# Pre-LN attention and binarized feed-forward on one core: probabilities weigh the normalised rows, projection last, rows turned by DMA and VectorE

## Chip, cores and metric

One NeuronCore of a Trainium2 chip runs the whole program. The metric is the device time of one execution in microseconds (us), lower is better. TensorE is called PE below (PEld is its weight load), VectorE DVE, ScalarE ACT, GpSimd POOL, SyncE SP (the engine that issues most DMAs).

## The reference, cut to what matters

```python
def attn(x, Wq, bq, Wk, bk, Wv, bv, Wo, bo):          # x is the layer-normed input
    Q, K, V = x @ Wq.T + bq, x @ Wk.T + bk, x @ Wv.T + bv
    s = einsum('bqd,bkd->bqk', Q, K) / sqrt(d) * gaussian_mask   # a factor per key
    return einsum('bqk,bkd->bqd', softmax(s), V) @ Wo.T + bo
def ffn(x, w1, b1, w2, b2):                            # alpha = mean |w| of a row
    h = gelu(x @ (alpha1 * sign(w1)).T + b1)           # exact gelu
    return h @ (alpha2 * sign(w2)).T + b2
x = x + attn(layernorm(x), ...)
x = x + ffn(layernorm(x), ...)       # x: 16 x 1024 x 256 float32, hidden 1024
```

## The kernel before

There are B = 16 batches of S = 1024 tokens with D = 256 features. Token p*8+t lies in partition p of row tile t, so T = 8 tiles of 128 tokens make a batch, in N2 = 2 halves of TH = 4. C = 2 chunks of 128 features, J = 8 chunks of 128 hidden units. All products run in fp32r, and the precision comes from splitting an operand into a high part (a rounded copy, names with h) and a low part (value minus high, names with l): three products hi*hi, hi*lo, lo*hi, or two where the other side is a sign.

Weights are folded once: M = Wq.T Wk (scores are x M x.T) and N = Wv.T Wo.T (values and output projection in one). Per batch:

- `turn_rows` (PE, L840) transposes the normalised rows into PSUM; ACT and DVE split them into xh, xl (`hi_rows`, `lo_rows`), DVE makes the masked keys from the same PSUM (`mask_keys`, L589), ACT and POOL split these (`hi_keys`, `split_keys` L315).
- `queries` (L856 to L859) and `values` (L873 to L875, rows times N).
- `scores` (L889) of one query tile over all keys; DVE takes the row maximum (`row_max`, L609), ACT the exponential (L447) into the buffer prob, SP issues four DMAs that exchange blocks of 32 partitions (`regroup_probs`), DVE finishes the transpose in 32x32 blocks (`turn_probs`, L615), ACT makes pth (`hi_probs`, L460), POOL ptl (`lo_probs`, L322).
- `weigh_values` (L907 to L909) for each query tile: 24 products with the probabilities as weights, 256 or 258 columns; the two columns more are ones and give the sum of the probabilities. DVE divides and adds (`add_attention`), takes the statistics, POOL the rstd (`rstd_ffn`), ACT normalises again (`normalize_ffn`).
- `turn_rows_ffn` (L935), hi and lo parts (L643), the first feed-forward layer (L1075) by hidden chunk over all 1024 tokens, gelu (ACT, L552) into one of three slots of g, `split_column` (DVE: a copy L648 into gh, a subtraction L650 into gl), the second layer `ffn_rows` (L927, L928), `scale_outputs` (DVE, L668), `add_ffn` (POOL, L340), store.

The order on every engine is written out by hand in a function `batch` per engine; engines meet only at semaphores, and an engine does nothing out of order. Batches overlap: the scores of batch b+1 run between the feed-forward rows of batch b. In `batch` of PE the eight chunks of the first layer stand together and are followed by `scores(b + 1, 0)`. POOL's order behind the last `rstd_ffn` is `add_b2` (eight additions, L334), then `add_ffn` in turn with `add_bias` of the next batch (L328).

## Time and profile before

| what | value |
|---|---|
| median of 3 runs | 1490.33 us (1489.58 to 1492.18) |
| span of the profiled execution (first to last instruction) | 1486.6 us |
| PE busy | 1460.9 us, 98% of the span |
| DVE, ACT, POOL busy | 1030.6, 787.6, 835.7 us (69%, 53%, 56%) |
| chain that ended last | PE 91% of the span |
| mean granted TensorE clock | 0.995 of full speed |

The span is that of one execution that the profiler recorded; it has no run time of its own beside it, and stands 3.7 us under the median of the other three. The chain of waits is followed back from the last instruction, so its shares say which engine set the time where. Matmuls are pipelined: a matmul's own duration is longer than the distance from one to the next, and the distance is what it costs.

### The profile page before, as it was taken

How to read it: one execution, taken by the hardware profiler on the slowest of the kernel's cores; microseconds unless marked ns; L12 is line 12 of the kernel's file. 1: busy time of each engine (PE TensorE's matmuls, PEld its weight loads, DVE VectorE, ACT ScalarE, POOL GpSimd, SP SyncE). 2: the span in 40 equal slices, each digit the busy share in tenths (PEclk: the TensorE clock that was granted, in tenths of full speed). 3: DMA queues.
4: the chain of work that ended last, by engine and by line, in shares of the span. 5: the costliest groups of instructions: out<-in, count | busy, mean ns of one | idle time of the engine just before them, and what ended most of it. 6: DMA issues, size and time to landing. Idle time of an engine off the chain costs nothing.

```text
span 1486.6 us, 24033 instructions
## 1 busy us (share of the span) xinstructions
PE 1460.9 (98%) x9421; PEld 1327.1 (89%) x9421; DVE 1030.6 (69%) x1681; ACT 787.6 (53%) x951; POOL 835.7 (56%) x1097
## 2 busy tenths in 40 slices
PE   8999999999999999999999999999999999999997
PEld 6889989999898998989999898998989999899986
DVE  7567776767767667776776767677675777767574
ACT  5564654646556464654646556465564646546341
POOL 3564637556374673637656375673646746375553
PEclk9999999999999999999999999999999999999999
DMA  5312412223121332403214122231303224121220
GB/s 191 81 34 43 128 27 75 71 57 114 36 76 60 71 100 43 123 19 73 86 48 124 29 71 72 65 106 44 100 29 82 89 44 128 25 75 44 57 86 29
DMA packets 86060, 106.16 MB, mean 71 GB/s; under 512 B 9390, under 2 KB 77372, under 8 KB 85948
## 3 DMA queue, kind: packets, MB, share of 16 engines
q1 hardware_dynamic: 85920, 104.63, 25.0%
q8 instruction: 74, 1.21, 0.4%
q14 instruction: 38, 0.31, 0.1%
q10 hardware_dynamic: 28, 0.01, 0.0%
HBM read 20.72 MB, written 16.78 MB: 25 GB/s over the span
## 4 chain that ended last, share of the span: by engine, by line
PE 91%; DMA 2%; DVE 2%; ACT 2%; SPq 1%; issue 1%; POOL 1%; POOLq 0%
PE ps L889 22%; PE ps L1075 15%; PE ps L927 8%; PE ps L928 8%; PE ps L907 7%; PE ps L909 7%; PE ps L908 7%; PE ps L873 2%; PE ps L874 2%; PE ps L875 2%; PE ps L935 2%; PE ps L856 2%; PE ps L857 2%; PE ps L859 2%; PE ps L840 2%; DMA prob<-prob 2%
## 5 line engine op out<-in xcount | busy, mean ns | idle before, releaser
L322 POOL TENSOR_TENSOR ptl<-pt,pth 128x512 fp32r<-128x512 f32 x256 | 327.1, 1299 | 188.3 <-ACT pth L460 188.3
L907 PE MATMUL ps<-vh,pth 128*128 128x258 f32 x1024 | 293.6, 287 | 2.9 <-POOL ptl L322 2.9
L340 POOL TENSOR_TENSOR xin<-xin,ys 128x256 f32<-128x256 f32 x128 | 94.6, 740 | 353.4 <-DVE ys L668 353.3
L909 PE MATMUL ps<-vh,ptl 128*128 128x258 f32 x1024 | 288.9, 282 | 0.0
L908 PE MATMUL ps<-vl,pth 128*128 128x256 f32 x1024 | 288.4, 282 | 0.0
L460 ACT ACTIVATE pth<-pt 128x1024 fp32r<-128x1024 f32 x128 | 135.8, 1061 | 251.2 <-DVE pt L615 251.1
L927 PE MATMUL ps<-sgn,gh 128*128 128x256 f32 x1024 | 248.6, 284 | 6.1 <-DVE gl L650 6.1
L928 PE MATMUL ps<-sgn,gl 128*128 128x256 f32 x1024 | 248.5, 284 | 0.0
L609 DVE TENSOR_REDUCE nmax<-ps 128x1 f32<-128x1024 f32 x128 | 156.5, 1223 | 120.1 <-PE ps L889 120.1
L447 ACT ACTIVATE prob<-ps,nmax 128x1024 f32<-128x1024 f32 x128 | 142.8, 1115 | 181.6 <-DVE nmax L609 181.4
L615 DVE STREAM_TRANSPOSE pt<-prob 128x1024 f32<-128x1024 f32 x128 | 158.8, 1241 | 67.4 <-DMA prob<-prob 67.2
L927 PEld LDWEIGHTS ps<-sgn,gh 128*128 128x128 f32 x1024 | 197.4, 193 | 7.9 <-issue 6.7
L907 PEld LDWEIGHTS ps<-vh,pth 128*128 128x128 f32 x1024 | 194.2, 190 | 7.4 <-issue 3.3
L908 PEld LDWEIGHTS ps<-vl,pth 128*128 128x128 f32 x1024 | 195.6, 191 | 3.7
L928 PEld LDWEIGHTS ps<-sgn,gl 128*128 128x128 f32 x1024 | 197.5, 193 | 1.2
L909 PEld LDWEIGHTS ps<-vh,ptl 128*128 128x128 f32 x1024 | 195.0, 190 | 0.0
L552 ACT ACTIVATE g<-ps,cols,alpha 128x1024 f32<-128x1024 f32 x120 | 145.2, 1210 | 64.2 <-PE ps L1075 63.6
L889 PE MATMUL ps<-kh,qh 128*128 128x512 f32 x512 | 159.2, 392 | 1.8 <-ACT sgn L430 1.8
L650 DVE TENSOR_TENSOR gl<-g,gh 128x1024 fp32r<-128x1024 f32 x128 | 157.8, 1233 | 4.4
L889 PE MATMUL ps<-kl,qh 128*128 128x512 f32 x512 | 158.7, 391 | 0.0
L889 PE MATMUL ps<-kh,ql 128*128 128x512 f32 x512 | 158.3, 390 | 0.0
L1075 PE MATMUL ps<-x2h,sgn 128*128 128x512 f32 x480 | 154.7, 393 | 0.3
(116 smaller groups left out, 2798.0 us busy)
## 6 DMA issues: line engine op xcount, KB each, us to landing
prob<-prob SPq DMA_DIRECT2D x512, 128.0 KB, 3.1
xin<-in_L_attn_x_dram SPq DMA_DIRECT2D x32, 512.0 KB, 4.5
out_dram<-xin SPq DMA_DIRECT2D x31, 512.0 KB, 3.8
w1s<-in_L_ffn_w_dram SPq DMA_DIRECT2D x1, 1024.0 KB, 10.0
w2s<-in_L_ffn_w_dram SPq DMA_DIRECT2D x1, 1024.0 KB, 12.0
mask_bc<-mask_dram SPq DMA_DIRECT2D x1, 512.0 KB, 7.1
out_dram<-xin SPq DMA_DIRECT2D x1, 384.0 KB, 2.4
wk<-in_L_attn_Wk_dram SPq DMA_DIRECT2D x1, 256.0 KB, 4.8
```

The lines of the kernel that those rows point to most:

```text
L322: pool.tensor_tensor(ptl[:, q % P_SLOTS, half(n)], pt[:, q % P_SLOTS, half(n)], pth[:, q % P_SLOTS, half(n)].bitcast(F32), ALU.subtract).t ...
L552: act.activation(two(g[:, j % G_SLOTS, :]), slot(2 - j % 2), ACT.Gelu, bias=cols[:, j:j + 1], scale=alpha1[:, j:j + 1]).then_inc(gelu_set, 1)
L609: dve.tensor_reduce(nmax[:, q:q + 1], slot(q % 2), mybir.AxisListType.XY, ALU.max, negate=True).then_inc(max_set, 1)
L615: dve.transpose(pt[:, q % P_SLOTS, :].rearrange("p (j g c) -> p g j c", j=T, c=QUAD), regrouped(q).rearrange("p (g j r) -> p g j r", j=T, ...
L650: dve.tensor_tensor(lo, val, hi.bitcast(F32), ALU.subtract).then_inc(gl_set, 1)
L889: last = pe.matmul(ps[:, 2 * (q % 2) + n, :], part[:, c, tile(q)], keys[:, c, half(n)], start=c == 0 and part is qh and keys is kh, stop=c ...
L907: pe.matmul(with_sum, pth[:, q % P_SLOTS, tile(j)], vh[:, j, 0:D + 2], start=j == 0, stop=False)
L908: pe.matmul(bank, pth[:, q % P_SLOTS, tile(j)], vl[:, j, :], start=False, stop=False)
L909: last = pe.matmul(with_sum, ptl[:, q % P_SLOTS, tile(j)], vh[:, j, 0:D + 2], start=False, stop=j == T - 1)
L927: pe.matmul(bank, gh[:, t, j, :], sgn2[:, j, :], start=j == 0, stop=False)
L928: last = pe.matmul(bank, gl[:, t, j, :], sgn2[:, j, :], start=False, stop=j == J - 1)
L1075: last = pe.matmul(ps[:, 4 - 2 * (j % 2) + n, :], sgn1[:, c, tile(j)], x2l[:, n, c, :] if lo else x2h[:, c, half(n)], start=c == 0 and not ...
```

## The change

**Attention.** The values disappear: `weigh_rows` weighs the normalised rows themselves (xnh, xnl as weights, the probabilities of four query tiles as 512 moving columns), and `project` multiplies the result with N afterwards. The sums of the probabilities come from the exponential's accumulator (rsum).

**Rows.** The normalised rows are no longer turned by PE. POOL normalises the rows of batch b+2 (`normalize_attention`), SP issues eight DMAs that regroup them (`regroup_rows`), DVE turns them in 32x32 blocks into SBUF (`turn_rows`). `lo_rows` and `mask_keys` of DVE now read this SBUF copy in place of PSUM, and several operations write or read with a step of four elements (`from_quads`). POOL gets `lo_values` (the low part of the rows).

**Feed-forward.** The first layer goes by pairs of hidden chunks over half of the tokens (`hidden_pair`), the first half before the second half of the attention output is projected. The three slots of g hold both gelu outputs and exponentials, so that `exponentials(b + 1, 0)` waits until the last pair of batch b is split. The second layer uses banks of its own rows in `probs`.

Core of the diff:

```diff
@@ sync
+            def regroup_rows(b, n):
+                sp.wait_ge(xn1_set, T * b + TH * (n + 1))
+                if b == 1:
+                    sp.wait_ge(q_summed, QG)
+                else:
+                    sp.wait_ge(hidden, J * (b - 1))
+                for i in range(QUADS):
+                    sp.dma_start(regrouped_rows[i * QUAD:(i + 1) * QUAD, n, :],
+                                 xn1[:, n, i, :, :, :].rearrange("p c t k -> p (c t k)")).then_inc(rows_back[n], 16)
...
+                if b + 2 < B:
+                    for n in range(N2):
+                        load(b + 2, n)
+                    for n in range(N2):
+                        regroup_rows(b + 2, n)
+                if b + 1 < B:
+                    for q in range(TH):
+                        regroup_probs(b + 1, q)
@@ gpsimd
+            def normalize_attention(b):
...
+                    pool.tensor_scalar(xn1_tile(t), in_blocks(xin[s][:, t, :]), mv1[:, t, 0:1], rstd1[:, t:t + 1],
+                                       ALU.subtract, ALU.mult).then_inc(xn1_set, 1)
+            def lo_values(b):
+                for k in range(QG):
+                    n, c = divmod(k, C)
+                    pool.wait_ge(xnh_set, QG * b + k + 1)
+                    pool.tensor_tensor(rows_by_tile(xnl, n, c), xn1_by_tile(b, n, c),
+                                       rows_by_tile(xnh, n, c).bitcast(F32), ALU.subtract).then_inc(xnl_set, 1)
...
+                for q in tiles_of(1):
+                    rstd_ffn(b, q)
+                if more:
+                    lo_values(b + 1)
+                if b + 2 < B:
+                    normalize_attention(b + 2)
+                add_b2(b)
@@ scalar
             def exponentials(b, q):
                 act.wait_ge(max_set, T * b + q + 1)
-                if b > 0 or q >= 2:
-                    act.wait_ge(p_back[(q - 2) % QUEUED], 64 * ((T * b + q - 2) // QUEUED + 1))
+                if q >= G_SLOTS:
+                    act.wait_ge(p_back[(q - G_SLOTS) % QUEUED], 16 * QUADS * ((T * b + q - G_SLOTS) // QUEUED + 1))
+                elif b > 0:
+                    act.wait_ge(gl_set, J * b)
@@ vector
+            def turn_rows(b, n):
+                dve.wait_ge(rows_back[n], 16 * QUADS * b)
+                dve.wait_ge(kl_set, N2 * b)
+                dve.transpose(rows_t(n).rearrange("p (j g r) -> p g j r", g=QUADS, r=QUAD), ...
@@ tensor
+            def weigh_rows(b, n, steps):
+                parts = [(xv, lo, j) for j in range(T) for xv, lo in ((xnh, 0), (xnl, 0))]
+                parts += [(xnh, 1, j) for j in range(T)]
...
+                        pe.wait_ge(pth_set, T * b + TH * (n + 1))
...
+                        last = pe.matmul(ps[:, PV_BANK + c, :], xv[:, j, tile(c)],
+                                         probs[:, lo, first:first + TH, tile(j)],
+                                         start=k == 0, stop=k == len(parts) - 1)
...
+            def batch(b, more):
+                for i in range(TH):
+                    scores(b, TH + i)
+                    weigh_rows(b, 0, range(6 * i, 6 * i + 6))
+                if more:
+                    queries(b + 1)
+                project(b, 0, more)
+                weigh_rows(b, 1, range(0, 16))
+                turn_rows_ffn(b, 0)
+                weigh_rows(b, 1, range(16, 24))
+                hidden_pair(b, 0)
+                project(b, 1, more)
+                hidden_pair(b, 1)
+                hidden_pair(b, 2)
+                turn_rows_ffn(b, 1)
+                hidden_pair(b, 3)
+                if more:
+                    scores(b + 1, 0)
+                for k in range(4, J):
+                    hidden_pair(b, k)
...
+                scores(b + 1, 1)
+                ffn_row(b, 0, more)
+                ffn_row(b, 1, more)
+                scores(b + 1, 2)
+                ffn_row(b, 2, more)
+                ffn_row(b, 3, more)
+                scores(b + 1, 3)
+                for r in range(TH, T):
+                    ffn_row(b, r, more)
```

`queries(b + 1)` issues its four groups one behind the other into two banks, a group k >= 2 waits for `ql_set` of group k - 2, and `project(b, 0)` takes the same two banks. In the DVE order `row_max(b + 1, 1)`, two `scale_outputs`, `turn_probs(b + 1, 0)`, `row_max(b + 1, 2)`, ..., `turn_probs(b + 1, 2)`, `scale_outputs(b, 4)` follow the last split; `ffn_row(b, 6)` waits for `scale_outputs(b, 4)`.

How the instructions move on POOL, between the last rstd of a batch and the first addition of a feed-forward row. Before:

```order
L315 TENSOR_TENSOR kl<-kmf,kh 128x2x512
L304 TENSOR_TENSOR ve<-mv,eps 128x1
L306 TENSOR_TENSOR rstd<-ve,mhalf 128x1
L309 TENSOR_SCALAR nmr<-mv,rstd 128x1
L334 TENSOR_TENSOR xin<-xin,b_bc 128x256 x8
L340 TENSOR_TENSOR xin<-xin,ys 128x256
```

Now:

```order
L384 TENSOR_TENSOR ve<-mv,eps 128x1
L386 TENSOR_TENSOR rstd<-ve,mhalf 128x1
L389 TENSOR_SCALAR nmr<-mv,rstd 128x1
L365 TENSOR_TENSOR xnl<-xn,xnh 128x4x128 x4
L358 TENSOR_SCALAR xn<-xin,mv,rstd 128x8x32 x8
L402 TENSOR_TENSOR xin<-xin,b_bc 128x256 x8
L409 TENSOR_TENSOR xin<-xin,ys 128x256 x2
```

Twelve instructions (L365, L358) stand in front of the eight additions, and `add_bias` (L328) went to another place.

The same stretch on DVE, from the low part of the feed-forward rows to the next row maximum. Before (the last of the copies and subtractions follow in the same manner):

```order
L643 TENSOR_TENSOR x2l<-ps,x2h 128x1024 [waits x2h_set]
L604 TENSOR_TENSOR vl<-ps,vh 128x512 [waits vh_set]
L648 CAST gh<-g 128x8x128 [waits gelu_set,kl_set]
L650 TENSOR_TENSOR gl<-g,gh 128x8x128 [waits gh_set]
L648 CAST gh<-g 128x8x128 [waits gelu_set]
L650 TENSOR_TENSOR gl<-g,gh 128x8x128 [waits gh_set]
```

Now:

```order
L719 CAST probs<-g 128x2x4x128 [waits gelu_set]
L721 TENSOR_TENSOR probs<-g,probs 128x2x4x128 [waits gh_set]
L712 TENSOR_TENSOR rows_l<-ps,rows_h 128x1024 [waits x2h_set]
L719 CAST probs<-g 128x2x4x128 [waits gelu_set]
L721 TENSOR_TENSOR probs<-g,probs 128x2x4x128 [waits gh_set]
L719 CAST probs<-g 128x2x4x128 [waits gelu_set]
L721 TENSOR_TENSOR probs<-g,probs 128x2x4x128 [waits gh_set]
L677 TENSOR_REDUCE nmax<-ps 128x1 [waits scored]
L719 CAST probs<-g 128x2x4x128 [waits gelu_set]
L721 TENSOR_TENSOR probs<-g,probs 128x2x4x128 [waits gh_set]
```

The low part of the second half of the rows and the first row maximum of the next batch now stand among the copies and subtractions.

## Rows read from the trace of the kernel before

**Rows 1.** The page, part 1 and the clock line of part 2.

```profile
PE 1460.9 (98%) x9421; PEld 1327.1 (89%) x9421; DVE 1030.6 (69%) x1681; ACT 787.6 (53%) x951; POOL 835.7 (56%) x1097
...
PEclk9999999999999999999999999999999999999999
```

**Rows 2.** Timeline of DVE, start us and us, where two batches' splits begin.

```profile
738.39 0.69 DVE L648 CAST gh<-g 128x1024 fp32r<-128x1024 f32 x1 [2.02 <-ACT g L552]
...
740.26 0.69 DVE L648 CAST gh<-g 128x1024 fp32r<-128x1024 f32 x1
...
828.18 0.69 DVE L648 CAST gh<-g 128x1024 fp32r<-128x1024 f32 x1 [2.00 <-ACT g L552]
```

**Rows 3.** The chain of waits in order of time: start us, us, what.

```profile
106.43 13.90 PE ps L1075 x60
...
131.53 2.75 PE ps L889 x12
...
169.04 0.89 PE ps L840 x8
```

**Rows 4.** Timeline of PE: first and last of 23 matmuls of `weigh_values`.

```profile
775.88 0.28 PE L907 MATMUL ps<-vh,pth 128*128 128x258 f32 x1
...
778.50 0.28 PE L908 MATMUL ps<-vl,pth 128*128 128x256 f32 x1
```

**Rows 5.** Timeline: an exponential on ACT, the transpose of its row on DVE.

```profile
777.34 1.12 ACT L447 ACTIVATE prob<-ps,nmax 128x1024 f32<-128x1024 f32 x1 [3.26 <-DVE nmax L609]
...
783.54 1.25 DVE L615 STREAM_TRANSPOSE pt<-prob 128x1024 f32<-128x1024 f32 x1 [0.63 <-DMA prob<-prob]
```

**Rows 6.** Groups of instructions: busy us, mean ns of one, idle before.

```profile
L322 POOL TENSOR_TENSOR ptl<-pt,pth 128x512 fp32r<-128x512 f32 x256 | 327.1, 1299 | 188.3 <-ACT pth L460 188.3
L650 DVE TENSOR_TENSOR gl<-g,gh 128x1024 fp32r<-128x1024 f32 x128 | 157.8, 1233 | 4.4
L609 DVE TENSOR_REDUCE nmax<-ps 128x1 f32<-128x1024 f32 x128 | 156.5, 1223 | 120.1 <-PE ps L889 120.1
L334 POOL TENSOR_TENSOR xin<-xin,b_bc 128x256 f32<-128x256 f32 x128 | 89.8, 740 | 11.4 <-ACT xn L509 10.8 <-DVE xn L638 0.6
L648 DVE CAST gh<-g 128x1024 fp32r<-128x1024 f32 x128 | 87.9, 687 | 31.5 <-ACT g L552 30.1 <-ACT g L493 1.5
L315 POOL TENSOR_TENSOR kl<-kmf,kh 128x1024 fp32r<-128x1024 f32 x32 | 79.7, 2492 | 17.0 <-ACT kh L406 17.0
L306 POOL TENSOR_TENSOR rstd<-ve,mhalf 128x1 f32<-128x1 f32 x128 | 72.6, 567 | 10.0
L596 DVE SCALAR_TENSOR_TENSOR ql<-ps,ccol,qh 128x512 fp32r<-128x512 f32 x64 | 46.5, 747 | 22.4 <-ACT qh L395 22.4
L395 ACT ACTIVATE qh<-ps,ccol 128x512 fp32r<-128x512 f32 x64 | 42.0, 680 | 28.4 <-PE ps L859 28.4
L583 DVE TENSOR_TENSOR xl<-ps,xh 128x1024 fp32r<-128x1024 f32 x32 | 38.4, 1202 | 0.5 <-ACT xh L389 0.5
L309 POOL TENSOR_SCALAR nmr<-mv,rstd 128x1 f32<-128x1 f32 x128 | 34.6, 270 | 12.6
```

**Rows 7.** One batch by stretches: us, then busy us of PE, PEld, DVE, ACT, POOL.

```profile
739.60:829.90 90.30, 90.28 (x588) 82.32 (x587) 63.62 (x104) 49.59 (x59) 51.57 (x68) 1.00 0.24 71
739.60:750.00 10.40, 10.40 (x47) 8.61 (x46) 10.23 (x12) 6.78 (x7) 0.00 (x0) 1.00 0.00 0
```

**Rows 8.** Timeline in the last batch, POOL and DVE at work together.

```profile
1444.81 0.69 DVE L648 CAST gh<-g 128x1024 fp32r<-128x1024 f32 x1
...
1444.90 3.98 POOL L322 TENSOR_TENSOR ptl<-pt,pth 128x512 fp32r<-128x512 f32 x2
...
1445.53 2.20 DVE L650 TENSOR_TENSOR gl<-g,gh 128x1024 fp32r<-128x1024 f32 x1
```

**Rows 9.** Stretches around PE's first long wait; behind POOL's column the granted clock.

```profile
47.90:50.80 2.90, 0.06 (x1) 0.01 (x1) 2.90 (x7) 2.17 (x2) 1.39 (x2) 0.91 0.31 50
50.90:53.50 2.60, 2.60 (x12) 2.60 (x13) 1.43 (x9) 1.06 (x1) 2.03 (x3) 0.50 0.31 101
```

More of the change, by code:

```diff
@@ L845, in queries @@
-            def queries(b, groups, first=False):
-                for k in groups:
+            def queries(b):
+                for k in range(QG):
                     n, m = divmod(k, C)
@@ new lines, in project @@
+            def project(b, n, more):
+                yh, yl = y_part(0, n), y_part(1, n)
+                pe.wait_ge(yh_set, N2 * b + n + 1)
+                for i, q in enumerate(tiles_of(n)):
+                    if i % 2 == 0:
+                        if n > 0:
+                            pe.wait_ge(x1_set, T * b + TH)
+                        elif more:
+                            pe.wait_ge(ql_set, QG * (b + 1) + 3 + i // 2)
+                        else:
+                            pe.wait_ge(ffn_scaled, T * b)
+                    at = order_in_half(n).index(q)
+                    bank = ps[:, QO_BANK + i // 2, (i % 2) * D:(i % 2 + 1) * D]
+                    for k, (part, N) in enumerate(((yh, Nh), (yh, Nl), (yl, Nh))):
+                        if i == 0 and part is yl:
+                            pe.wait_ge(yl_set, N2 * b + n + 1)
+                        for c in range(C):
+                            last = pe.matmul(bank, part[:, c, tile(at)], N[:, c, :], start=k == 0 and c == 0,
+                                             stop=k == 2 and c == C - 1)
+                    last.then_inc(o_summed, 1)
@@ L934, in turn_rows_ffn @@
+            def turn_rows_ffn(b, n):
+                pe.wait_ge(xn2_set, T * b + TH * (n + 1))
+                if n == 0:
+                    pe.wait_ge(exp_set, T * b + T - 1)
+                else:
+                    pe.wait_ge(yl_set, N2 * (b + 1))
+                for t in tiles_of(n):
                     for c in range(C):
[L935 removed]
+                        last = pe.transpose(ps[:, (0 if n == 0 else PV_BANK) + c, tile(t % TH)], xn2(t)[:, tile(c)],
+                                            ident[:])
@@ new lines, in ffn_row @@
+            def ffn_row(b, r, more):
+                bank = ps[:, QO_BANK + r % 2 if more else PV_BANK + r % 2, 0:D]
+                if r == 0 and more:
+                    pe.wait_ge(gelu_set, J * (b + 1))
+                if r % TH == 0:
+                    pe.wait_ge(gl_set, J * b + (J // N2) * (r // TH + 1))
+                if r >= 2:
+                    pe.wait_ge(ffn_scaled, T * b + r - 1)
+                for j in range(J):
+                    pe.matmul(bank, probs[:, 0, r, tile(j)], sgn2[:, j, :], start=j == 0, stop=False)
+                    last = pe.matmul(bank, probs[:, 1, r, tile(j)], sgn2[:, j, :], start=False, stop=j == J - 1)
+                last.then_inc(ffn_summed, 1)
```

1153 lines of the change are left out of this document (540 added, 613 removed).

## The prediction

> **What bounds the kernel now.** The busy shares come first: PE is busy for 98% of the span and its clock is full throughout [rows 1]. A busy PE can still be a waiting PE, so the next view is the distance from batch to batch. The splitting of the hidden layer on DVE begins at 738.39 and at 828.18 in two batches that follow each other [rows 2]: a period of 89.8 us. Against it stands PE's own work, from the distances between its matmuls: 12 of 512 columns in 2.75 us, 0.229 each, 8 transposes in 0.89, 60 of the first layer in 13.90 [rows 3], and 22 distances of 256 or 258 columns in 2.62 us, 0.119 each [rows 4]. Per batch that makes scores 8 x 2.75 = 22.0, weighing 192 x 0.119 = 22.9, first layer 64 x 0.232 = 14.8, second layer 128 x 0.12 = 15.4, values 48 x 0.12 = 5.8, queries 24 x 0.232 = 5.6, four groups of transposes 3.5: 90.0 us. PE's work is the period. Everything that shortens PE's list helps; everything that makes PE wait costs in full.
>
> **PE's list after the change.** Weighing becomes 96 matmuls of 512 columns in place of 192 of 256: 96 x 0.229 = 22.0, 0.9 less. The 16 transposes of the rows leave PE: 1.8 less. The columns of ones leave with them. `project` is the 48 matmuls of `values` in another place, and scores, queries and both layers have the same counts. 90.0 - 2.7, set against the measured 89.8, leaves **87.2 us of work**: if nothing waited, 15 periods would give 39 us. That is the whole gain to be had. The question is what PE now waits for, and I follow one batch with the durations of the rows. Time zero is the end of the first half of the weighing.
>
> **Queries, 2.0 us.** Four groups run one behind the other in two banks. At 0 ACT still copies the probabilities of tile 6; then it takes the high part of the weighed rows (as long as an exponential, 1.12 [rows 5], for the same 1024 columns), then the first queries (0.68 [rows 6]), until 3.1. DVE needs 1.20 for the low part of the weighed rows and 0.75 for the low part of the queries [rows 6]: 4.5. PE has finished two groups at 2.8 and waits 1.7. `project` then waits some 0.3 for the same banks, because the transpose of tile 7 stands in front of the third low part on DVE. Before, weighing lay between the groups and hid this. Bounds: 0 if ACT comes early, 3 if the strided outputs are slower than contiguous ones.
>
> **Turns and bank of the second half, 2.2 us.** `turn_rows_ffn` comes twice, each time behind four additions with statistics on DVE, a chain of three small instructions on POOL (the longest 567 ns [rows 6]) and a normalisation on ACT; the cover is 7.2 us of weighing at first, and hidden pairs 1 and 2 (3.7 us) the second time. By hand it is short by 0.6 each time; hidden pair 2 waits 0.9 for the bank of `project(b, 1)`, and 0.1 is lost at the low part. Bounds 0 and 4.
>
> **The splits, 6.7 us, the largest term.** In the old order POOL does nothing while DVE splits (0.00 busy in that stretch [rows 7]). Now POOL has 20 instructions there: 4 subtractions of 512 columns at 1.30, 8 normalisations, 8 additions at 0.74 (0.70 apart) [rows 6]. The normalisation has no row on POOL; it lies between the same instruction for one column, 270 ns, and the addition with two inputs, 740 [rows 6]; I take 0.6, nearer to the addition, which has the same number of columns. Together 15.6 us. What happens when both work is in [rows 8]: the cast runs from 1444.81 to 1445.50, POOL's two subtractions, issued at 1444.90, take 3.98 instead of 2 x 1.30, and DVE's subtraction from 1445.53 takes 2.20 instead of 1.23. They take turns: DVE waited for the first half of POOL's work, POOL's second half for DVE. Only these forms do so; a row maximum or a transpose is as long beside POOL as alone. The Trainium skill says the same (SBUF — State Buffer, "Who interferes with whom"): a DVE instruction in a two-port mode or with two SBUF inputs and a GpSimd instruction that reads SBUF exclude each other for a whole instruction. By that page `lo_rows` and `mask_keys` join too, since both inputs are in SBUF now; the rows agree for the cast and the subtraction.
>
> By hand: DVE is through with its additions at 31.5. A pair of cast and subtraction takes 1.87 [rows 2]. Without POOL eight of them, the low part of the second half (1.20) and one maximum (1.22 [rows 6]) end at 50.4, gelu waits included. With POOL the first three pairs lose little, since POOL itself waits for ACT's last copies of the rows until 39.3; the ten instructions of the last five pairs each meet one of POOL's, 2 x 1.30 + 8 x 0.65 = 7.8: the last split ends at 58.2. There the change ties a knot: the exponential of the next batch waits for that split, as g is shared, and ends at 59.4. PE has scores(b+1, 1) and two rows of the second layer to do and then needs it. It has waited 1.6 for the last gelu, whose slot is freed by a split, arrives at 54.3, and waits 5.1. Sum 6.7.
>
> **The chain behind it, 2.3 us.** From the end of an exponential to the transpose of its row 5.08 us pass (783.54 - 778.46 [rows 5]); four DMA issues and the transfer are in it. DVE's order makes it a chain: transfer 5.1, transpose 1.25, row maximum 1.2, exponential 1.1, transfer 5.1, transpose 1.25, scaling of row 4 0.4, 15.4 in all, and only then may `ffn_row(b, 6)` start. PE has 2 x 2.75 + 4 x 1.92 = 13.2 us of work meanwhile: a wait of 2.3 with rounding. Five microseconds without work also cost clock: after a wait of 2.9 the granted clock was 0.50, the lower level of 1.2 GHz, and 12 matmuls took 2.60 us instead of 1.43 [rows 9]. The 1.2 us fit into the 2.3, so they add nothing here.
>
> **Smaller edits.** Eight more DMAs a batch (rows of two batches ahead) stand in SP's queue in front of the first exchange of probabilities; in my walk the second half of the normalisation ends at 56, before the exponential at 59.4, so they cost nothing while that order holds. DVE's two transposes (2 x 1.25) replace the lower work on values and hide under weighing. The accumulator of the exponential adds a short read per tile on ACT, which is half idle. The sum over the last batch and the front (values out, waits in) I take as unchanged, plus or minus 5 us.
>
> One rule speaks against an edit that I priced at nothing. `split_keys` of POOL now reads with a step of 16 bytes, while the old one took 2.49 us with contiguous reads [rows 6]. The Trainium skill (GPSIMD Engine Reference, "Performance pitfalls for Q7 kernels") gives half as much again for reads with a step above 8 bytes; the two would take 1.2 us longer each, an estimate from that page and the row, and since they stand in front of the rstd chain the sum would be some 20 us more. No row here shows it.
>
> **Sum.** Waits of 2.0 + 2.2 + 6.7 + 2.3 = 13.2 on 87.2 make a period of 100.4; with DVE and POOL never in each other's way it is 93.0 (queries 2.0, turns 2.2, the chain 1.1, gelu 0.5). The turns of [rows 8] are measured in one place; not each of ten instructions will meet a full one, and I take 98.5. Fifteen periods at 98.5 - 89.8 = 8.7 give 130 us. The profiled execution's span is 1486.6, which becomes 1617; it stood 3.7 below the median of the other runs, so I forecast **1620 us**. Its own range, from 95.5 to 101.5 a period, is 1575 to 1665.
>
> **Rivals.**
> (1) *The waits stay hidden.* DVE and ACT run earlier than in my walk and PE keeps 98% busy. The time is 1490 - 15 x 2.3 = 1455. For it speaks that DVE and ACT are only about two thirds busy. It decides at a total wait of 2.6 us a batch: below it the change is faster. Against it: DVE instructions that exclude POOL (8 x 1.87 for the splits and four of 1.2, 20 us) and POOL's list (52 a batch now [rows 7], 10 more with 4 x 1.30 and 8 x 0.6) add up to 82 of 87 us. Chance 0.17.
> (2) *Chain without contention.* Period 93.0: 1490 + 15 x 3.2 = 1538. POOL's work would fall into the gaps of DVE. Slower all the same, by queries, turns and the chain. Chance 0.25.
> (3) *SP's queue.* POOL, slowed by DVE or by strided reads, normalises later than the last split; the rows' DMAs then hold back the first exchange. Each microsecond costs 15; from 3 us on the time is above 1665. Chance 0.05.
> (4) *No difference*: waits happen to fill just the 2.6 us. Chance 0.03.
> The forecast has 0.50.
>
> **Numbers.** A measurement of this kernel tells 0.2% from no change. Slower 0.50 + 0.25 + 0.05 = 0.80, same 0.03, faster 0.17. The range reaches from 1475 (part of case 1, where some of the gain is lost) to 1670; about 0.13 lies below and 0.05 above.
>
> **What would show it.** Right: the period from cast to cast is 95 to 101; casts and subtractions of the hidden layer have means well above 687 and 1233 ns, POOL's subtractions above 1299; PE idles in front of scores for the exponential, and in front of `ffn_row` for the scaling, with the granted clock below 0.99; the chain of waits is no longer nearly all PE's and holds DVE, ACT and the transfers of probabilities. Wrong: casts at 0.69 and PE's waits short (case 2 or 1), or a wait of SP for the normalisation in front of the first exchange (case 3). PE's work itself should be 87 us a batch; if matmuls of the weighing lie further apart than 0.229, that step fails.

## The result, and the profile after

| | before | after |
|---|---|---|
| median | 1490.92 us (4 runs, 1489.58 to 1492.18) | 1830.26 us (4 runs, 1821.73 to 1841.10) |
| ratio after/before | | 1.228, 95% interval 1.224 to 1.233 |
| span of the profiled execution | 1486.6 us | 1828.1 us |
| mean granted TensorE clock | 0.995 | 0.935 |

The change costs 339 us. I had forecast 130, with 1670 us as the upper end of the range. The direction was right, the size was wrong, and the time lies outside the range.

The head of the profile of the changed kernel, busy shares and slices of granted clock, against [rows 1]:

```profile
PE 1534.9 (84%) x7645; PEld 1290.1 (71%) x7645; DVE 1128.3 (62%) x1560; ACT 885.6 (48%) x1118; POOL 1243.6 (68%) x1281
PEclk8889998999999899999989988999999999989999
```

PE was busy for 98% of the span and is for 84%, and its clock, full before, is below 0.9 in nine of the slices. No other engine is above 68%, so none has become the bound by its amount of work. The question is where PE waits. Here is one batch by windows, from the first product behind the queries' wait to the same product a batch later (columns: us, busy time and count of PE, PEld, DVE, ACT, POOL, then granted clock, DMA share, GB/s), and under it the three stretches at the lower level of the clock:

```profile
873.96:986.53 112.57, 94.29 (x472) 79.29 (x473) 69.57 (x96) 54.55 (x68) 78.49 (x81) 0.94 0.31 66
...
873.96:877.00 3.04, 3.04 (x7) 2.44 (x8) 1.89 (x2) 0.11 (x1) 2.61 (x1) 0.50 0.61 172
943.82:948.50 4.68, 4.68 (x22) 4.68 (x23) 2.69 (x3) 3.02 (x5) 4.68 (x6) 0.50 0.29 88
952.34:955.30 2.96, 2.96 (x14) 2.96 (x15) 0.28 (x1) 0.73 (x1) 2.88 (x3) 0.50 0.10 12
```

PE's timeline over that batch: all rows with an idle time ahead of them (start, duration, engine, line, tiles; in brackets the idle time and what ended it).

```profile
880.79 0.51 PE L952 MATMUL ps<-Nh,probs 128*128 128x256 f32 x2 [0.62 <-DVE ql L670]
890.27 1.09 PE L964 MATMUL ps<-ident,probs 128*128 128x128 f32 x8 [0.50 <-ACT probs L517]
897.08 0.50 PE L952 MATMUL ps<-Nh,probs 128*128 128x256 f32 x2 [0.25 <-ACT probs L508]
899.14 0.74 PE L952 MATMUL ps<-Nh,probs 128*128 128x256 f32 x4 [1.32 <-DVE probs L690]
904.26 0.50 PE L982 MATMUL ps<-rows_h,sgn 128*128 128x512 f32 x1 [0.63 <-DVE xin L702]
908.44 1.09 PE L964 MATMUL ps<-ident,probs 128*128 128x128 f32 x8 [2.08 <-ACT probs L517]
929.68 0.74 PE L904 MATMUL ps<-kh,qh 128*128 128x512 f32 x2 [1.72 <-ACT g L498]
943.82 0.55 PE L995 MATMUL ps<-sgn,probs 128*128 128x256 f32 x1 [4.51 <-DVE ys L729]
952.34 0.58 PE L995 MATMUL ps<-sgn,probs 128*128 128x256 f32 x1 [2.32 <-DVE ys L729]
986.53 0.77 PE L884 MATMUL ps<-rows_h,Mh 128*128 128x512 f32 x1 [4.21 <-DVE ql L670]
```

The idle times sum to 18.2 us. Half of the 10.7 us at granted clock 0.50, 5.3 us, is what the lower level costs PE. That leaves 89.1: my 87.2 of work, and 1.9 which I put down, without having shown it, to the slow first product and its weights behind each of ten waits. A count that does not start from my sum says nearly the same: the median distance of each form of product in this batch (0.227 us for 512 columns, 0.12 for 256), times its count, adds up to some 86 us. Each stretch at 0.50, which is the level of 1.2 GHz, stands directly behind one of the three waits above 2.3 us; behind the shorter ones the granted clock stays at 1.00 (877 to 939 us).

Over the program the sum closes too. From one load of the gelu table to the next, the first 14 periods have a mean of 89.9 us before and 111.8 after (14 x 21.95 = 307 us); the last one has 71.6 and 100.9 (29 us), and the first load comes at 106.1 and 111.6 (5.5 us). Together 342 us, against spans that differ by 341.5.

Now the instructions whose durations I had assumed, in the view by groups (shapes, count, busy us, mean ns, idle time before), against [rows 6]:

```profile
L358 POOL TENSOR_SCALAR xn<-xin,mv,rstd 128x256 f32<-128x256 f32 x120 | 200.2, 1679 | 2.5 <-issue 2.4
L721 DVE TENSOR_TENSOR probs<-g,probs 128x1024 fp32r<-128x1024 f32 x128 | 183.9, 1436 | 4.4
L719 DVE CAST probs<-g 128x1024 fp32r<-128x1024 f32 x128 | 106.5, 832 | 48.6 <-ACT g L540 48.6
L402 POOL TENSOR_TENSOR xin<-xin,b_bc 128x256 f32<-128x256 f32 x128 | 98.0, 800 | 0.7 <-ACT probs L517 0.7
L371 POOL TENSOR_TENSOR kl<-probs,kh 128x1024 fp32r<-128x1024 f32 x32 | 95.8, 2995 | 84.0 <-ACT kh L483 84.0
L690 DVE TENSOR_TENSOR probs<-ps,probs 128x1024 fp32r<-128x1024 f32 x32 | 64.5, 2015 | 102.3 <-ACT probs L508 102.3
L508 ACT ACTIVATE probs<-ps 128x1024 fp32r<-128x1024 f32 x32 | 63.2, 1976 | 17.9 <-PE ps L929 17.9
```

Two surprises stand here. A normalisation on POOL takes 1.68 us in the mean, where I had bounds of 0.27 and 0.74. And the parts that are written with a step of four elements (L508, L690) take 2.0 us on ACT and on DVE, where the same 1024 columns took 1.12 and 1.23.

The mean of 1.68 hides two values. Here is one normalisation beside the splits and the last two of the same batch, behind the last split:

```profile
921.85 2.03 POOL L358 TENSOR_SCALAR xn<-xin,mv,rstd 128x256 f32<-128x256 f32 x1
...
929.41 2.42 POOL L358 TENSOR_SCALAR xn<-xin,mv,rstd 128x256 f32<-128x256 f32 x2
```

The 14 normalisations of the program beside which DVE is idle take 1.22 us each. Those that lie beside a cast or a subtraction of the splits for nearly all of their time take 1.95 in the mean. So the form is slow by itself, and taking turns with the splits adds 0.7 again.

At the seam of two batches SP's queue shows what the first did. SP's timeline, then DVE's first transpose of probabilities:

```profile
925.93 8.41 SPq L294 DMA_DIRECT2D regrouped_rows<-xn  x8
934.43 47.74 SPq L284 DMA_DIRECT2D probs<-g  x32
```

```profile
940.99 1.25 DVE L685 STREAM_TRANSPOSE probs<-probs 128x1024 f32<-128x1024 f32 x1 [10.86 <-DMA probs<-g]
```

The first exponential ended at 929.53. Its exchange was not issued before 934.43, since the rows' eight DMAs stood in front and POOL's normalisation ended only at 931.8. This is the picture of my rival (3), to which I had given 0.05. An estimate from these rows: eight normalisations of 1.22 us would have ended at 927.9, before that exponential.

### The profile page after: what moved, and what is told of

The parts are those of the page before. It is cut to its first block and busy times, and to the rows that moved or that the text cites. A ratio compares the mean times of both kernels' runs of the same rounds, so it can differ in the third digit from the quotient of the medians.

```text
span 1828.1 us, 20907 instructions
## 1 busy us (share of the span) xinstructions
PE 1534.9 (84%) x7645; PEld 1290.1 (71%) x7645; DVE 1128.3 (62%) x1560; ACT 885.6 (48%) x1118; POOL 1243.6 (68%) x1281
## 5 line engine op out<-in xcount | busy, mean ns | idle before, releaser
L379 POOL TENSOR_TENSOR probs<-probs 128x512 fp32r<-128x512 f32 x256 | 351.2, 1390 | 162.9 <-ACT probs L504 162.2
L995 PE MATMUL ps<-sgn,probs 128*128 128x256 f32 x1024 | 284.8, 311 | 99.0 <-DVE ys L729 99.0
L995 PEld LDWEIGHTS ps<-sgn,probs 128*128 128x128 f32 x1024 | 222.7, 217 | 110.5 <-issue 72.6
L929 PE MATMUL ps<-probs,xnh 128*128 128x512 f32 x1024 | 283.6, 391 | 0.0
L996 PE MATMUL ps<-sgn,probs 128*128 128x256 f32 x1024 | 279.7, 306 | 0.0
L996 PEld LDWEIGHTS ps<-sgn,probs 128*128 128x128 f32 x1024 | 222.4, 217 | 0.8
L929 PEld LDWEIGHTS ps<-probs,xnh 128*128 128x128 f32 x1024 | 190.0, 188 | 38.0
L982 PE MATMUL ps<-rows_h,sgn 128*128 128x512 f32 x512 | 208.0, 406 | 8.6 <-DVE xin L702 6.9
L540 ACT ACTIVATE g<-ps,cols,alpha 128x512 f32<-128x512 f32 x256 | 183.3, 775 | 62.0 <-PE ps L982 47.4
L982 PE MATMUL ps<-rows_l,sgn 128*128 128x512 f32 x512 | 203.6, 398 | 0.0
L358 POOL TENSOR_SCALAR xn<-xin,mv,rstd 128x256 f32<-128x256 f32 x120 | 200.2, 1679 | 2.5 <-issue 2.4
L721 DVE TENSOR_TENSOR probs<-g,probs 128x1024 fp32r<-128x1024 f32 x128 | 183.9, 1436 | 4.4
```

The lines of the kernel that those rows point to most:

```text
L358: pool.tensor_scalar(xn1_tile(t), in_blocks(xin[s][:, t, :]), mv1[:, t, 0:1], rstd1[:, t:t + 1], ALU.subtract, ALU.mult).then_inc(xn1_set, 1)
L379: pool.tensor_tensor(ptl(q)[:, half(n)], pt(q)[:, half(n)], pth(q)[:, half(n)].bitcast(F32), ALU.subtract).then_inc(ptl_set, 1)
L540: last = act.activation(g[:, k % G_SLOTS, half(m)], ps[:, PAIR_BANK[k] + m, :], ACT.Gelu, bias=cols[:, j:j + 1], scale=alpha1[:, j:j + 1])
L721: dve.tensor_tensor(hidden_part(1, n, js), val, hidden_part(0, n, js).bitcast(F32), ALU.subtract).then_inc(gl_set, 1)
L929: last = pe.matmul(ps[:, PV_BANK + c, :], xv[:, j, tile(c)], probs[:, lo, first:first + TH, tile(j)], start=k == 0, stop=k == len(parts) - 1)
L982: last = pe.matmul(ps[:, PAIR_BANK[k] + m, :], sgn1[:, c, tile(j)], part[:, n, c, :], start=c == 0 and part is rows_h, stop=c == C - 1 and ...
```

## Experiments

Line numbers in the experiments' rows are shifted by their edits; the tile names are the same.

**e1: the rows' DMAs behind two exchanges.**

```diff
-                    for n in range(N2):
-                        regroup_rows(b + 2, n)
-                if b + 1 < B:
-                    for q in range(TH):
-                        regroup_probs(b + 1, q)
+                for q in range(TH):
+                    if q == 2 and b + 2 < B:
+                        for n in range(N2):
+                            regroup_rows(b + 2, n)
+                    if b + 1 < B:
+                        regroup_probs(b + 1, q)
```

> Only SP's order changes: the eight DMAs that regroup the rows of two batches ahead are issued behind the exchanges of the first two tiles of probabilities instead of in front of them. Queue theory: in the changed kernel the first exchange is issued 4.9 us after its exponential ended, because SP waits for the second half of the normalisation; now it is issued at once, DVE's wait of 10.9 us before the first transpose falls to about 5, and PE's waits in front of the second layer's rows 4 to 7 (4.5 + 2.3 us a batch) fall by 4 to 6 us, with some of the matmuls at the lower clock behind them: 15 x (4 to 7) = 60 to 105 us, so 1725 to 1770 us. Rival, splits and chain (the exponentials come late because of DVE's splits, and the exchange behind them is long in itself): PE's waits stay within 1 us a batch, 1815 to 1835 us.

Measured: 1832.37 us, ratio to the kernel before 1.227 (1.223 to 1.232). No gain at all. SP's timeline, and the transpose of tile 2 on DVE:

```profile
936.80 5.12 SPq L284 DMA_DIRECT2D probs<-g  x8
942.02 5.06 SPq L294 DMA_DIRECT2D regrouped_rows<-xn  x8
947.21 7.17 SPq L284 DMA_DIRECT2D probs<-g  x8
```

```profile
956.80 1.25 DVE L686 STREAM_TRANSPOSE probs<-probs 128x1024 f32<-128x1024 f32 x1 [7.12 <-DMA probs<-g]
```

The first exchange is now issued at once and lands 5.9 us behind its exponential. But the exponential of tile 2 ended at 946.05, and its probabilities were there only at 956.8, 10.8 us later: the eight transfers of rows are now in front of that one. 1.2 us of it is SP, which was still issuing them (946.05 to 947.21), and 9.6 are from the issue to the transpose, where the first exchange took 5.8 (936.80 to 942.55). Over the inner batches the probabilities of tile 2 come 10.7 us behind their exponential in e1, and 5.8 in e9 below, where these DMAs do not exist. PE had 4.51 + 2.32 us of waits there and has 0.13 + 7.11. The DMAs were not hidden by being put later, they were moved in front of another exchange. I had named the delay rightly and taken the place for the cause.

**e2: a normalisation without blocks.**

```diff
-                    pool.tensor_scalar(xn1_tile(t), in_blocks(xin[s][:, t, :]), ...
+                    pool.tensor_scalar(xn1_tile(t), xin[s][:, t, :], ...
```

(and `xn1_tile` gives 256 columns in one piece)

> POOL's normalisation reads and writes its 256 columns in one piece each; it no longer puts them into blocks of 32 in the order of the regrouping, so the rows that attention sees from batch 1 on are in a wrong order. Everything else is the changed kernel. Block theory: the 1.68 us of one normalisation come from reading or writing in blocks; it takes 0.6 to 0.8 us, eight end some 7 us earlier, before the exponential, SP issues the first exchange at once, and the time is that of the kernel with the rows' DMAs behind, 1725 to 1770 us, or somewhat less. Rival, the instruction is slow on POOL in this form (two scalars per partition): 1.6 to 1.7 us as before, 1820 to 1840 us.

Measured: 1829.47 us, ratio 1.227 (1.225 to 1.230), and by groups:

```profile
L358 POOL TENSOR_SCALAR xn<-xin,mv,rstd 128x256 f32<-128x256 f32 x120 | 198.2, 1662 | 2.5 <-issue 2.4
```

The block theory is out: in one piece the instruction is as slow, 1.22 us alone and 1.94 beside the splits. What remains is the form (1.22) and DVE's splits beside it. In the changed kernel its shortest is 1.21 us, the longest 2.68. The addition with two inputs, 740 ns for the same columns [rows 6], was no bound for it.

**e3: high and low parts without the step.** `from_quads` writes in the order of `in_quads`.

```diff
-            return ap.rearrange("p (t r g) -> p t g r", g=QUADS, r=QUAD)
+            return ap.rearrange("p (t g r) -> p t g r", g=QUADS, r=QUAD)
```

> The high and low parts of rows, keys and attention outputs are written in the order in which they are read, without the step of four elements, on ACT, DVE and POOL; the tokens then stand in another order than they should inside each tile of 128. Step theory: ACT's three forms fall from 1.98 to 2.06 us to 1.03, DVE's low parts from 2.0 to 1.2, POOL's split of the keys from 3.0 to about 2.5; the wait for the queries, 4.2 us a batch, falls by 1.7, the matmuls at the lower clock behind it by up to 1.5 us: 1770 to 1805 us. Rival, the parts are hidden and the wait is made by the order of the instructions alone: the wait stays above 3.7 us and the time at 1820 to 1835 us.

Measured: 1745.41 us, ratio 1.171 (1.168 to 1.174), 85 us less than the changed kernel and more than I expected. By groups:

```profile
L371 POOL TENSOR_TENSOR kl<-probs,kh 128x1024 fp32r<-128x1024 f32 x32 | 76.5, 2392 | 39.4 <-ACT kh L483 39.4
L690 DVE TENSOR_TENSOR probs<-ps,probs 128x1024 fp32r<-128x1024 f32 x32 | 39.2, 1225 | 71.6 <-ACT probs L508 71.6
L508 ACT ACTIVATE probs<-ps 128x1024 fp32r<-128x1024 f32 x32 | 32.5, 1017 | 17.9 <-PE ps L929 17.9
```

```profile
940.76 0.47 PE L884 MATMUL ps<-rows_h,Mh 128*128 128x512 f32 x1 [2.37 <-DVE ql L670]
```

The second fence is PE's timeline: the queries' wait falls from 4.21 to 2.37 in this batch (2.87 in the next), and the products behind it are at granted clock 1.00. Both waits inside `project` for the stepped parts (0.25 and 1.32 above) are gone as well. So a step of 16 bytes costs 0.96 us on ACT per 1024 columns, where the output has it, 0.79 on DVE and 0.60 on POOL (2.99 against 2.39, a quarter more), where the output and one of the two inputs have it. Which of the two operands costs was not run. The Trainium skill (GPSIMD Engine Reference, "Performance pitfalls for Q7 kernels") gives half more on POOL for reads with a step above 8 bytes; the runs show a quarter more, with one of two inputs stepped. Its page "SBUF — State Buffer" (section "Door 1: The DMA port swizzle") says that SBUF has lines of 16 bytes and that each access that crosses to a new line pays a penalty; the direction fits the step of 16 bytes here, and the size stands only in the rows. The same place counts a stride of 4 fp32 as free; at exactly that stride these rows are slower.

**e4: PE's waits filled with idle products.**

```diff
+                    if k == 2 and b > 0:
+                        pe.wait_ge(exp_set, T * (b - 1) + T - 1)
+                        for _ in range(FILL - 2):
+                            pe.matmul(ps[:, 0, :], sgn1[:, 0, 0:P], sgn2[:, 0:2, :], start=True, stop=True)
...
+                if r == TH and more:
+                    for _ in range(FILL):
+                        pe.matmul(ps[:, PV_BANK, :], sgn1[:, 0, 0:P], sgn2[:, 0:2, :], start=True, stop=True)
```

(`FILL` is 18)

> PE gets idle work in two places where it waits: 16 products of 512 columns into a free bank between the second and the third group of the queries, and 18 in front of row 4 of the second layer; nothing reads them. Clock theory: the granted clock falls to 0.50 in these waits and PE pays for it behind them, 7 matmuls of the queries at 0.43 us instead of 0.23 and 22 of the rows 4 and 5 at 0.21 instead of 0.12. With the waits filled the distances are 0.23 and 0.12 from the start. At the queries that is won (1.4 us a batch, 20 us in all); at rows 4 and 5 the 2.1 us only lengthen the wait in front of row 6, which is set by a scaling behind a transfer. So 1800 to 1820 us. Rival, the matmuls there are slow for another reason (operands just written, the engine's restart): the distances stay at 0.43 and 0.21, and the time at 1825 to 1840 us.

Measured: 1850.26 us, ratio 1.241 (1.238 to 1.245). PE's timeline at the queries and, in another batch, in the second layer:

```profile
891.34 0.50 PE L889 MATMUL ps<-rows_h,Mh 128*128 128x512 f32 x1 [0.70 <-DVE ql L671]
891.68 0.39 PE L890 MATMUL ps<-rows_l,Mh 128*128 128x512 f32 x1
891.91 0.40 PE L889 MATMUL ps<-rows_h,Mh 128*128 128x512 f32 x1
...
848.86 0.38 PE L1003 MATMUL ps<-sgn,probs 128*128 128x256 f32 x1 [1.99 <-DVE ys L730]
849.09 0.28 PE L1004 MATMUL ps<-sgn,probs 128*128 128x256 f32 x1
...
850.57 0.41 PE L1004 MATMUL ps<-sgn,probs 128*128 128x256 f32 x1
850.78 0.41 PE L1003 MATMUL ps<-sgn,probs 128*128 128x256 f32 x1
```

At the queries the clock theory holds: the distances behind the filled wait are 0.23 us from the second one on, where they were 0.43. In the second layer it does not hold as I put it. A wait of 1.99 remained, the products began at 0.12 and fell to the lower level 1.5 us after PE had started again (0.21 apart, granted clock 0.50 from 850.4 to 853.5), and the wait ahead of row 6 was 2.5 us in this batch and 4.0 in the next. So the lower clock can also arrive while PE is busy, and filling a wait with nothing useful gained nothing, although the mean granted clock rose from 0.935 to 0.948. Why the whole became 20 us slower I cannot say from these rows; that stays open.

**e7: the normalisation on ACT**, behind the exponential of tile 1, with the rows' DMAs as in e1.

```diff
-                if b + 2 < B:
-                    normalize_attention(b + 2)
...
+                    act.activation(xn1_tile(t), in_blocks(xin[s][:, t, :]), ACT.Identity, bias=nmr1[:, t:t + 1],
+                                   scale=rstd1[:, t:t + 1]).then_inc(xn1_set, 1)
```

> The normalisation of the rows of two batches ahead leaves POOL and goes to ACT, behind the exponential of tile 1, as eight activations of 256 columns (POOL makes their bias with two small instructions), and SP issues the rows' DMAs behind the exchanges of two tiles. POOL theory: moving the DMAs alone gave nothing because POOL is late as a whole: its eight normalisations (12.7 us) hold back the additions of b2 and of rows 0 and 1, which free the two buffers of the scaling, so that the scaling of row 2 waited for POOL. Without them the additions end before 932, a normalisation on ACT takes 0.6 us, and PE's waits in front of rows 4 to 7 fall from 7.1 us a batch to 1 to 3: with the clock 5 to 8 us a batch, 1710 to 1760 us. Rival, the transfers set it (exponential, exchange, transpose, maximum, whatever POOL does): the waits stay above 5 us, 1800 to 1835 us.

Measured: 1864.15 us, ratio 1.251 (1.249 to 1.254). POOL has 12.7 us a batch less to do beside the splits, and the kernel is 32 us slower than e1: neither theory had that. POOL's timeline and two of DVE's rows beside it:

```profile
938.62 11.36 POOL L410 TENSOR_TENSOR xin<-xin,b_bc 128x256 f32<-128x256 f32 x8
```

```profile
943.67 1.23 DVE L737 CAST probs<-g 128x1024 fp32r<-128x1024 f32 x1
944.93 1.64 DVE L739 TENSOR_TENSOR probs<-g,probs 128x1024 fp32r<-128x1024 f32 x1
```

The additions of b2, which had come behind the last split, now come beside the splits. Eight take 11.4 us instead of 5.6, and a pair of cast and subtraction 2.82 us, against 2.02 to 2.10 beside the normalisation in the changed kernel. That is the taking of turns of [rows 8]. The additions lose more than the normalisation did and cost DVE more.

**e8: e7 with the additions behind the last split.**

```diff
                 pool.wait_ge(xn2_set, T * (b + 1))
+                pool.wait_ge(gl_set, J * (b + 1))
                 for t in range(T):
                     pool.tensor_tensor(xin[s][:, t, :], xin[s][:, t, :], b2_bc[:], ALU.add).then_inc(b2_added, 1)
```

> The kernel with the normalisation on ACT, and POOL's eight additions of b2 now wait until the last pair of the hidden layer is split. Lock theory: that kernel was 32 us slower than the changed one although POOL had less to do, because its additions (two inputs) came beside the splits and took turns with them (11.4 us for eight instead of 5.6, a pair of cast and subtraction 2.85 us instead of 2.1), where the normalisation had left the splits alone. With the additions behind the splits a pair takes 1.9 to 2.1 us, the last split ends 3 to 4 us earlier, and 45 to 60 us are won: 1800 to 1820 us. Rival, the 32 us come from the exchange of tile 2, late behind the rows' transfers and behind the normalisation on ACT: the pairs may be shorter, the time stays at 1850 to 1870 us.

Measured: 1815.99 us, ratio 1.218 (1.216 to 1.220). One wait added, 48 us gained. By groups:

```profile
L738 DVE CAST probs<-g 128x1024 fp32r<-128x1024 f32 x128 | 100.0, 782 | 50.2 <-ACT g L557 50.2
L411 POOL TENSOR_TENSOR xin<-xin,b_bc 128x256 f32<-128x256 f32 x128 | 89.6, 738 | 148.4 <-DVE probs L740 148.4
```

The mean of the additions falls from 1382 (e7) to 738 ns and that of the casts from 1004 to 782. That the two take turns, and that this made e7 slow, is shown. Against e1, from which e8 differs by the normalisation on ACT and by this wait, 16 us are gained. The Trainium skill (SBUF — State Buffer, "Who interferes with whom") says that a cast in a two-port mode excludes any GpSimd read of SBUF for a whole instruction; the additions agree. Beside POOL's scalar form in the changed kernel the casts ran at 0.68 us and the subtractions at 1.38 instead of 1.23, while POOL's instructions took 1.95 beside the splits and 1.22 alone. So there the loss fell on POOL and hardly on DVE, and a subtraction and a normalisation do not exclude each other for a whole instruction.

**e9: no DMAs for the rows.** DVE transposes the blocks where they lie, so the exchange between partitions is left out; SP does not wait for the normalisation.

```diff
-                        regroup_rows(b + 2, n)
...
-                dve.wait_ge(rows_back[n], 16 * QUADS * b)
+                dve.wait_ge(xn1_set, T * b + TH * (n + 1))
```

> The changed kernel without the regrouping of the rows: SP issues none of these eight DMAs a batch and doesn't wait for the normalisation, and DVE transposes the 32x32 blocks of the normalised rows as they lie in their own partitions, so that attention from batch 1 on sees wrong rows. POOL's normalisation stays. Transfer theory: the eight DMAs cost what they hold back, first as issues (5.1 to 8.4 us of SP) and, put behind, as transfers in front of the third exchange (its first transpose came 10.9 us after its exponential, where the first one needs 5.9). Without them the first exchange lands 5 to 6 us after the exponential, and PE's waits in front of rows 4 and 6, 6.8 us a batch, fall to 2 to 3, near the 2.3 that I had predicted for this chain; with the clock 5 to 7 us a batch, 1725 to 1755 us. Rival, POOL theory: the scaling of row 2 waits for POOL's additions behind the normalisation whatever SP does; the waits stay above 5 us and the time above 1800 us.

Measured: 1746.91 us, ratio 1.172 (1.170 to 1.174), 83 us less than the changed kernel with POOL's normalisation as slow as ever (1654 ns). PE's timeline at rows 4 and 6 of the second layer:

```profile
903.17 0.36 PE L991 MATMUL ps<-sgn,probs 128*128 128x256 f32 x1 [0.17 <-DVE ys L725]
909.34 0.39 PE L991 MATMUL ps<-sgn,probs 128*128 128x256 f32 x1 [2.11 <-DVE ys L725]
```

6.8 us of waits have become 2.3 in this batch, and 2.6 in the mean of the inner batches, close to the chain that I had worked out without SP's queue. POOL theory falls, transfer theory stands: with e1 it says that the eight DMAs cost some 4.5 us of waiting and some clock a batch in both places that were tried.

**e5 and e6: two changes of order alone.** e5 takes two groups of queries in front of the last quarter of the weighing; e6 puts DVE's row maximum of tile 2 and its scalings ahead of the transposes, and ACT's exponential of tile 2 ahead of the copy of tile 0. Of both, one engine's edit is shown; in e5 the orders on ACT and DVE follow.

```diff
                     scores(b, TH + i)
+                    if more and i == TH - 1:
+                        queries(b + 1, range(0, 2))
                     weigh_rows(b, 0, range(6 * i, 6 * i + 6))
                 if more:
-                    queries(b + 1)
+                    queries(b + 1, range(2, QG))
```

> Two of the four groups of the queries move in front of the last quarter of the weighing; their high and low parts on ACT and DVE stand in front of those of the attention output. Order theory: the wait of 4.2 us for the first group's low part comes from its place behind both parts of the output; it goes to under 0.5, some 1.5 to 2.5 us appear in front of the projection, and the matmuls at the lower clock go too: 3 to 5 us a batch, 1755 to 1785 us. Rival, slack: the stretch behind is held by another chain (additions, statistics, POOL, gelu, splits), and what is won here is waited for in front of the second layer: 1815 to 1835 us.

Measured: 1807.46 us, ratio 1.213 (1.209 to 1.217), 23 us gained where 45 to 75 were expected.

```diff
-                turn_probs(b + 1, 0)
                 row_max(b + 1, 2)
                 scale_outputs(b, 2, more)
-                turn_probs(b + 1, 1)
+                turn_probs(b + 1, 0)
                 scale_outputs(b, 3, more)
+                turn_probs(b + 1, 1)
                 row_max(b + 1, 3)
-                turn_probs(b + 1, 2)
                 scale_outputs(b, 4, more)
+                turn_probs(b + 1, 2)
```

> DVE's order at the seam of two batches: the row maximum of tile 2 and the scalings of rows 2, 3 and 4 move one transpose ahead each, and ACT takes the exponential of tile 2 before the copy of tile 0's probabilities. SP's and POOL's order is that of the changed kernel. In-order theory: PE waits in front of rows 4 and 6 only because a scaling stands behind a transpose that waits for a transfer; the sum of the two waits, 6.8 us a batch, falls to 2 to 4 us, with the clock 4 to 6 us a batch, 1740 to 1775 us. Rival, POOL (the scaling of row 2 waits for an addition behind the normalisation): the first wait stays near 4 us, 1800 to 1835 us.

Measured: 1797.42 us, ratio 1.208 (1.204 to 1.212), 33 us gained where 55 to 90 were expected. Both land between their theories, and for the same reason: the wait that goes is partly waited for elsewhere. In e5 the queries' 4.8 become 2.1 in front of the projection, but the turn behind it waits 2.5 instead of 0.5 and the second layer 5.0 + 2.7. In e6 the 6.8 become 0.5 + 1.1 + 3.0, and the weighing waits 1.9 for the last exchange.

**c1: all orders and the normalisation on ACT; c2: c1 with the rows' transfers apart.** In both, the exponentials of tiles 0 and 2 wait only for the split that frees their own buffer. In c1 all eight DMAs stand between the exchanges of tiles 2 and 3; in c2 the first half is normalised earlier and stands in front of the first exchange, the second half in that place, and the additions of b2 come behind the last split. SP's edit of c2:

```diff
+                    if q in (0, 3) and b + 2 < B:
+                        regroup_rows(b + 2, q // 3)
+                    if b + 1 < B:
+                        regroup_probs(b + 1, q)
```

> All together: queries early, normalisation on ACT (half of it behind the exponential of tile 1, half behind the copy of tile 0), DVE's maxima and scalings ahead of the transposes, the rows' DMAs behind three exchanges, and the exponential of tiles 0 and 2 waits only for the split that frees its own buffer. If the waits are additive (18 us a batch: 4.8 queries, 4.8 between projection and the first layer, 1.7 exponential, 6.8 scaling; 7 us of lower clock), 12 us of waits and 6 of clock go: 1550 to 1590 us. If one chain through the batch holds it whatever the order: above 1650 us.

> The combined kernel (queries early, normalisation on ACT, maxima and scalings ahead of the transposes) with the rows' two halves apart: the first half is normalised in front of pair 4 and its DMAs stand before the first exchange, the second half's DMAs stand between the exchanges of tiles 2 and 3; the additions of b2 wait for the last split. The transfer theory has the fourth exchange, which landed 9.5 us after its exponential behind eight DMAs, land after 6 to 7; PE's wait of 5 us in front of the weighing falls to 1 to 2, with the clock 4 to 6 us a batch, 1675 to 1705 us. If the exchange is slow for itself, or the splits' place decides: 1740 to 1770 us.

Measured: c1 1766.70 us, ratio 1.186 (1.184 to 1.189), far above the 1550 to 1590 of waits that simply add up; c2 1659.74 us, ratio 1.113 (1.111 to 1.115), better than expected. PE's timeline where c1 had the weighing wait, in c1 and then in c2:

```profile
924.93 1.19 PE L950 MATMUL ps<-probs,xnh 128*128 128x512 f32 x2 [4.96 <-ACT probs L510]
```

```profile
871.63 0.70 PE L950 MATMUL ps<-probs,xnh 128*128 128x512 f32 x2 [0.31 <-ACT probs L510]
```

The fourth exchange landed 9.4 us behind its exponential in c1 and 5.8 in c2. c2's first 14 periods have a mean of 100.0 us, and its granted clock is 0.96. Of the 107 us between c1 and c2 the additions of b2 have a part too (e8: 48 us); the parts were not run alone. c2 beats the changed kernel by 170 us and is still 11% slower than the kernel before, so no version here is faster than the kernel before.

## Why the prediction was wrong, point by point

- **PE's list, 87.2 us of work: held.** Products of the weighing lie 0.227 apart, and the count by median distances gives some 86.
- **Queries, 2.0 us (0 to 3): measured 4.8**, above my upper bound. I had named the stepped outputs as the reason for the bound and then allowed one microsecond for it; e3 shows 1.8 us in the first wait alone. Apart from POOL's `split_keys`, which I put at 1.2 us more each outside the sum and which e3 shows at 0.60, the strided outputs are priced nowhere else: e3 shows 85 us in the whole.
- **Turns and bank of the second half, 2.2 us (0 to 4): measured 4.8** (0.50, 0.25, 1.32, 0.63, 2.08). 1.6 of them are the stepped parts in front of and inside `project(b, 1)`; the turns were short by 2.6, not 1.2.
- **Splits, 6.7 us, my largest term: measured 1.7.** The last split ended at 61.4 in my walk's time (928.32 - 866.89), forecast 58.2; the exponential at 62.6, forecast 59.4. That is near, but by luck. PE had by then waited 5.4 us more than forecast, at the queries and the turns, so it waited less here; and of the 7.8 us that DVE was to lose to POOL it lost 2.8 (eight casts at 832 ns instead of 687, eight subtractions at 1436 instead of 1233). Turns are taken, but I had put the loss on DVE, and the normalisation bore it (1.95 us instead of 1.22). With the additions, which the slow normalisation had pushed out of the stretch, DVE does lose (e7, e8).
- **The chain behind it, 2.3 us: measured 6.8.** This is the step that failed, and the sentence is in "Smaller edits": eight more DMAs cost nothing "while that order holds", with a normalisation ending at 56. At 1.7 us each in this batch instead of 0.6 it ended at 65. But e1 shows that the order alone was not it: the transfers need their time on the queue (tile 2's probabilities 10.7 us behind their exponential, 5.8 without them). Without them e9 gives 2.3 to 2.6, and the kernel is 83 us faster. The other large miss is the strided outputs under the queries and the turns, 85 us (e3).
- **Clock, nothing: measured 5.3 us a batch.** I had let it vanish inside a wait of 2.3 that ends on DVE's time. In the closed sum it stands as a term of its own, 1.5 of it behind the queries' wait and 3.8 in the second layer. How much full clock there would give back is not shown: e4 removed it at the queries and was not faster.
- **Front and last batch, unchanged within 5 us: measured 5.5 and 7.3 us more** (29.3 less 22.0).
- **Rival (3)** had the right queue and "above 1665" as its time. I gave it 0.05, since it needed a slow POOL, and I had bounded the one POOL instruction without a row by two rows that were both too short. But its condition, the wait for the normalisation, is not what costs the time: e1 takes it away and stays at 1832.
- **The sum.** I had taken 98.5 where my own terms gave 100.4. The misses in this batch are 1.9 for that, +2.8 queries, +2.6 turns, -5.0 splits, +4.5 chain, +5.3 clock and +1.9 left over: 14.0, and 98.5 + 14.0 = 112.5 against 112.57. An overestimate of 5.0 hid part of the rest.

The two terms, 85 us for the stepped parts (e3) and 83 for the rows' transfers (e9), would bring 1830 to 1662 if they add up. That they do was not run.

## What to carry to other kernels

An instruction form that the trace has never shown on that engine is not bounded by other forms of the same size; leave its upper end open, and ask which rival comes true there. A transfer added to a queue in which each transfer is waited for has no free place: look at what else is in flight until the next wait, not only at who issues first. And when PE's waits go from none to ten, price the clock behind each long one, because PE is slow just when it should catch up; whether that costs the whole is a question for a run.

## What I had not expected of the hardware

- POOL's subtract-and-multiply with two scalars per partition takes 1.22 us for 128x256 with DVE idle and 1.95 beside DVE's splits, whether in blocks of 32 or in one piece (means of 1679 and 1662 ns), while the addition of two such tiles takes 0.74.
- Writing fp32 with a step of 16 bytes nearly doubles an instruction of 1024 columns on ACT (1017 to 1976 ns). On DVE, with the second input stepped as well, it adds nearly two thirds (1225 to 2015).
- Less work on POOL made the kernel 32 us slower (e1 to e7), because a neighbour beside which a pair of cast and subtraction takes 2.0 us was replaced by one beside which it takes 2.8.
- The granted clock fell to 0.50 also 1.5 us after PE had resumed work behind a wait of 1.99 us (e4).
